# A four-layer graph network on one core: the gather lists are copied inside SBUF, and ScalarE takes over issues of SyncE

## What is computed

```
def _mp_layer(x, src_f, dst_f, ea_f, W, b):
    m = jnp.concatenate([x[dst_f], x[src_f], ea_f], axis=1) @ W.T + b
    agg = jax.ops.segment_sum(m, dst_f, num_segments=n)
    return jax.nn.relu(agg)
```

## Time and profile before

| | |
|---|---|
| runs shown | 19621.43, 19653.47, 19695.85 us; median 19653.47 |
| the profiled execution's own time | 19688.76 us |
| its span | 19687.0 us |
| TensorE clock granted, mean | 0.608 of full speed |
| busy | POOL 59%, PE 43%, DVE 24%, ACT 6% |
| first and last gather start | 723.4 us, 19640.2 us |

### The profile page before, as it was taken

One profiled execution on the slowest core, in us unless ns is written; L12 is line 12 of the kernel. 1 busy time (PEld: TensorE's weight loads), 2 busy tenths in 40 slices (PEclk: granted clock), 3 DMA queues, 4 the chain that ended last, 5 costly groups with the idle time before them and its releaser, 6 DMA issues.

```text
span 19687.0 us, 144709 instructions
## 1 busy us (share of the span) xinstructions
PE 8408.0 (43%) x34014; PEld 7081.4 (36%) x34014; DVE 4696.8 (24%) x7726; ACT 1131.3 (6%) x2610; POOL 11661.9 (59%) x11663
## 2 busy tenths in 40 slices
PE   7655555444443333334444443333323333333333
PEld 4334433333333333334444433333323333233333
DVE  4333333333342111112333321111111111211111
ACT  2101111000000000001111100000000000000000
POOL 0366665567776666655555556566556655466665
PEclk9877777677776555556766765555555555555555
DMA  4444444333332111113333321111111111111111
GB/s 195 153 127 151 151 143 139 110 99 99 100 100 59 27 30 30 29 37 90 91 91 92 92 57 24 23 24 24 22 27 24 24 23 23 26 24 26 26 26 25
DMA packets 1013134, 1320.33 MB, mean 67 GB/s; under 512 B 546589, under 2 KB 704574, under 8 KB 987470
## 3 DMA queue, kind: packets, MB, share of 16 engines
q0 software_dynamic: 426240, 764.57, 16.1%
q1 hardware_dynamic: 586830, 555.05, 8.8%
HBM read 970.98 MB, written 347.67 MB: 67 GB/s over the span
## 4 chain that ended last, share of the span: by engine, by line
another core or an unknown queue 55%; PE 16%; issue 15%; DVE 6%; POOL 3%; DMA 1%; SPq 1%; ACT 1%; DVEq 1%; ACTq 0%; POOLq 0%
PE PS L768 9%; PE PS L688 4%; POOL BIG L609 3%; DVE BIG L1366 1%; DVE OH L1353 1%; PE PS L801 1%; DMA AG<-acc 1%; PE PS L697 1%; PE PS L762 1%; DVE BIG L1373 1%; PE PS L675 0%; DVE BIG L1381 0%; ACT STG L969 0%; DVE XC L1221 0%
## 5 line engine op out<-in xcount | busy, mean ns | idle before, releaser
L768 PE MATMUL PS<-BIG,OH 128*128 128x64 f32 (+3 forms) x23310 | 5750.7, 427 | 3954.7 <-issue 1337.2
L609 POOL DMA_INDIRECT BIG<-t_mp,IDX x4995 | 4842.8, 970 | 3238.9 <-issue 1819.5
L768 PEld LDWEIGHTS PS<-BIG,OH 128*128 128x128 f32 x23310 | 5062.8, 295 | 4510.7 <-issue 2778.6
L609 POOL DMA_INDIRECT BIG<-t_cell,IDX x3330 | 3578.2, 1075 | 2546.6 <-issue 1799.1
L1353 DVE TENSOR_TENSOR OH<-REL,IOTA 128x640 f32<-128x640 f32 x2331 | 1902.3, 823 | 3537.9 <-remote 2841.7
L762 PE MATMUL PS<-STG,CARRY 128*128 128x64 f32 (+3 forms) x1554 | 554.2, 454 | 5100.0 <-ACT STG L969 3497.7
L609 POOL DMA_INDIRECT BIG<-t_p,IDX x1665 | 1618.0, 972 | 1192.9 <-issue 470.3
L762 PEld LDWEIGHTS PS<-STG,CARRY 128*128 128x128 f32 x1554 | 345.7, 277 | 5286.6 <-ACT STG L969 3460.7
L609 POOL DMA_INDIRECT BIG<-t_gcn,IDX x1665 | 1621.7, 974 | 1000.0 <-DMA IDX<-in_src 507.7
L1366 DVE TENSOR_TENSOR BIG<-BIG,COEF 128x1280 f32<-128x1280 f32 x666 | 990.7, 1488 | 511.9 <-DMA BIG<-t_cell,IDX 491.8
L801 PE MATMUL PS<-BIG 128*128 128x128 f32 x3330 | 585.0, 338 | 949.0 <-DVE BIG L1373 736.8
(11 more groups left out here) (148 smaller groups left out, 3345.1 us busy)
## 6 DMA issues: line engine op xcount, KB each, us to landing
t_cell<-BIG SPq DMA_DIRECT2D x198, 1280.0 KB, 4.5
BIG<-in_dst_row SPq DMA_DIRECT2D x333, 240.0 KB
BIG<-t_mp,IDX POOLq DMA_INDIRECT x4995
BIG<-t_cell,IDX POOLq DMA_INDIRECT x3330
BIG<-t_gcn,IDX POOLq DMA_INDIRECT x1665
BIG<-t_p,IDX POOLq DMA_INDIRECT x1665
BIG<-in_ef SPq DMA_DIRECT2D x333, 80.0 KB
BIG<-t_q SPq DMA_DIRECT2D x333, 48.0 KB
```

The source lines that it names most:

```text
L609: nc.gpsimd.indirect_dma_start(to[:, j, :], None, table, bass.IndirectOffsetOnAxis(ap=IDX[:, s // CHUNKS, at:at + 1], axis=0)).then_inc(ga ...
L768: last = nc.tensor.matmul(WIN[:, 0:out_w], OH[:, s % CHUNKS, j * P:(j + 1) * P], src[:, j, :], start=False, stop=(s % CHUNKS == CHUNKS - 1 ...
```

## The change

- `CELLS` and `SRCS`, two new SBUF tensors of 128 x 1665 int32, hold all lists: `CELLS` is written by DVE where the cell indices were written in place before, `SRCS` by one more load of the prologue.
- ACT copies 15 columns of them to `IDX` (`copy_list`), three groups ahead, behind the staging of the window whose group had the slot. POOL waits for one semaphore, `list_ready`. SP's list loads are gone from the fast passes, with their waits for the gathers.
- `store_window` moves from SP to ACT, directly behind `copy_list`.
- `load_mlp` moves from SP to ACT, behind the relu of the chunk before.
- SP keeps coefficients, edge attributes, and the node work.
- ACT runs the first and the last unit of each pass written out (`edged_units`), as it did in the first and the mlp pass.
- DVE's one-hots and products are as before; their second operands stay in SBUF.

```
-                        load_list(g + AHEAD, (gi + AHEAD) % UNIT)
-                    if kind == "mlp" and not (last and s + AHEAD >= SLOTS):
...
-                        load_mlp(at + AHEAD, (c + AHEAD) % CHUNKS)
-                    if kind == "mlp" and c == 1 and not (first and gi == 0):
-                        store_window(g - 1)
-                    if kind != "mlp" and c == 2:
-                        store_window(g)
+                        load_coefficients(g + AHEAD, (gi + AHEAD) % UNIT)
...
-                            pool.wait_ge(idx_in[s // CHUNKS], 16 * (ub + u + 1))
+                            pool.wait_ge(list_ready, gb + u * UNIT + s // CHUNKS + 1)
...
+                def store_window(g):
+
+                    act.wait_ge(win_staged, gb + g + 2)
+                    hold(act)
+                    at = act.value_load(WBASE[0:1, bass.ds(g * CHUNKS, 1)], min_val=0, max_val=z.nodes)
+                    act.dma_start(acc[bass.ds(at, P), :], STG[:, 0:acc.shape[1]]).then_inc(sums_landed, 16)
+
+                def copy_list(g, to):
+
+                    nc.scalar.activation(IDX[:, to, :], lists[:, bass.ds(g * TILES, TILES)], copy
+                                         ).then_inc(list_ready, 1)
+
+                def load_mlp(c, to):
+                    act.dma_start(RR[to][0:QW, :], t["dst_row"][0:1, bass.ds(c * CT * P, CT * P)]
+                                 .to_broadcast([QW, CT * P])).then_inc(rr_in[to], 16)
+                    act.dma_start(SZ[to][QW:P, :], t["ef"][:, bass.ds(c * CT * P, CT * P)]).then_inc(ef_in[to], 16)
+                    at = act.value_load(WBASE[0:1, bass.ds(c, 1)], min_val=0, max_val=z.nodes)
+                    act.dma_start(QM[to][0:QW, :], t_q[bass.ds(at, QW), :]).then_inc(q_in[to], 16)
...
                     if c == CHUNKS - 1:
                         stage_window(g)
+                        if not last:
+                            copy_list(g + UNIT, s // CHUNKS)
+                        store_window(g)
...
                 def mlp_body(u, s, first, last):
...
+                    if not (last and s + AHEAD >= SLOTS):
+                        at = u * SLOTS + s
+                        if not (first and s == 0):
+                            act.wait_ge(oht_ready, at)
+                            act.wait_ge(hid_done, at)
+                            hold(act)
+                        load_mlp(at + AHEAD, (s + AHEAD) % CHUNKS)
                     if s % CHUNKS == 0 and not (first and s == 0):
-                        stage_window(u * UNIT + s // CHUNKS - 1)
+                        g = u * UNIT + s // CHUNKS - 1
+                        stage_window(g)
+                        if not (last and s > 0):
+                            copy_list(g + UNIT, (s // CHUNKS - 1) % UNIT)
+                        store_window(g)
```

More of the change, by code:

```diff
@@ L230, in gnn_program @@
         gathered = [sem(f"gathered{s}") for s in range(SLOTS)]
-        idx_in = [sem(f"idx_in{s}") for s in range(UNIT)]
+        list_ready, idx_in = sem("list_ready"), sem("idx_in")
         coef_in = [sem(f"coef_in{s}") for s in range(UNIT)]
@@ L459, in fast_pass, with load_coefficients @@
                 kind, table, width, acc = passes[n]
[L460 to L467, removed]
+                gb = z.groups * n
+                def load_coefficients(g, to):
+                    sp.dma_start(COEF[:, to, :], coef_d[:, bass.ds(g * TILES * 4, TILES * 4)]
+                                 ).then_inc(coef_in[to], 16)
                     if n == 0:
@@ L470, in load_list @@
                                      [:, bass.ds(g * TILES * CAT_E, TILES * CAT_E)]).then_inc(ea_in[to], 16)
[L472 to L484, removed]
                 def body(u, s, first, last):
[L487 to L490, removed]
+                    c, gi = s % CHUNKS, s // CHUNKS
+                    g = u * UNIT + gi
+                    if kind == "spline" and c == 0 and not (last and gi + AHEAD >= UNIT):
                         if not (first and gi == 0):
[L492 to L498, removed]
+                            sp.wait_ge(prod_ready, CHUNKS * (gb + g))
+                            hold(sp)
                             if n == 0:
@@ L501, in body @@
                                 hold(sp)
[L502 to L514 removed]
+                        load_coefficients(g + AHEAD, (gi + AHEAD) % UNIT)
                 def node(s, k):
                     node_slot(n, s, k, CREDIT_STORE + 16 * (gb + (k + z.lag) * UNIT - 1))
[L519 to L520 removed]
+                if kind == "spline":
+                    for g in range(AHEAD):
+                        load_coefficients(g, g)
                 end_phase(n)
@@ L524, in fast_pass @@
                         sp.dma_start(QM[c][QW:P, :], t["mw1"][2 * F:2 * F + FEAT_E, :]).then_inc(sem("mwe_in"), 16)
[L525 to L529, removed]
+                if kind == "spline":
+                    edged_units(sp, body, node)
+                else:
+                    with sp.Fori(0, z.steps - TAIL) as k:
+                        for s in range(SLOTS):
+                            node(s, k)
                 tail_steps(lambda s, k: node_slot(n, s, k, CREDIT_STORE + 16 * (gb + z.groups)))
@@ L547, in body @@
                         hold(sp)
[L548 removed]
+                    sp.dma_start(IDX[:, 0, 0:1], lists[:, bass.ds(i, 1)]).then_inc(idx_in, 16)
                     if not first:
@@ L597, in fast_pass @@
                 kind, table, width, acc = passes[n]
-                cb, ub = z.chunks * n, z.units * n
+                cb, gb = z.chunks * n, z.groups * n
                 with pool.Fori(0, z.units) as u:
@@ L955, in fast_pass @@
                 cb, gb, ub = z.chunks * n, z.groups * n, z.units * n
+                lists = CELLS if kind == "spline" else SRCS
                 def copy_attributes(g, gi, u):
```

24 lines of the change are left out of this document (16 added, 8 removed).

## The result

The changed kernel takes **18965.75 us** (median of 3 runs, 18942.91 to 18981.92) against 19653.47: a ratio of 0.9647, 95% interval 0.9614 to 0.9681, so 688 us less. The prediction was 19400, 253 less. The direction was right and the time lies in the range, but the gain is 2.7 times the forecast.

What follows compares the result with a forecast made beforehand. POOL's gathers and its stops for index lists were taken as the bound. 19689 - 490 + 160 + 80 + 5 = 19444, less 35 for the median of runs: 19400 us; range 18600 to 20050, the forecast's own 18950 to 19550.

Steps and rivals of the forecast that it cites:

- What bounds the kernel: POOL's gathers, standing still for index lists: 2802 us in 280 stops, one being 6.8 us until the count, then 4.65.
- Lists by ACT's copy: Lists copied on ACT instead of loaded by SP: -490 us outside the mlp pass, +160 us in it.
- The 60% kept: Share of the 810 us from 222 shorter stops expected to remain, the rest lost to new stops; also applied to mlp.
- Store by ACT: 777 window stores, 1.26 us each, moved from SP to ACT behind the list copy, unseen by POOL: 0 us.
- Loads of the mlp pass by ACT: Three loads per chunk moved to ACT, 1.95 us, on the path at PE's 40 relu waits: +80 us.
- ACT's sequencer is slowed as SP's is: Rival: ACT issuing DMAs while POOL gathers becomes slow, mainly in mlp: 20340 us, or 20050 for mlp alone; chance 0.23 (with high mlp terms).
- Nothing is kept: Rival: PE's late counts set POOL's standing time, so shorter stops bring more stops: 19740 us, no change; chance 0.22.
- SP's slowness was the deadline: Rival: slow SP list loads cause the stops, and half of the 2802 us go: 18500 us; chance 0.13.
- The Trainium skill's rule: Issuing DMAs on several engines saves only sequencer time; only the list transfer counts, making the first term -215 us.
- More in number: Sign of being right: POOL's stops for lists become shorter but more numerous.
- shorter by 60 to 100 us each: Sign of being right: the time each sum pass loses.
- ACT's register instructions over 100 ns: Sign of being wrong, pointing to the rival of a slowed ACT sequencer.

Runs made afterwards that it cites:

- e1: Kernel before with only the list copies moved to ACT; window stores and mlp loads stay on SP: 19124.1 us, 0.9839 of the kernel before.
- e4b: Changed kernel plus two unread 1150-column copies on ACT between staging and list copy, on a chip with late counts: 19361.3 us, 0.9942 of the kernel before.
- e2: Changed kernel with only the window's store put back on SP: 19137.2 us, 0.9843 of the kernel before.
- e3: Changed kernel with only the mlp pass's loads put back on SP: 18840.3 us, 0.9697 of the kernel before.
- e10b: Changed kernel with the store on SP, in spline and sum passes issued behind the node step's load of the sums: 18869.3 us, 0.9696 of the kernel before.
- e0: The changed kernel run again, unaltered, as yardstick on another chip: 18848.2 us, 0.9688 of the kernel before.
- e6: Kernel before, with SP loading the list ahead of the previous group's store in spline and sum passes: 19031.0 us, 0.9665 of the kernel before.
- e7: Changed kernel plus two semaphore increments nobody waits for in each SP node slot: 19047.4 us, 0.9670 of the kernel before.
- e11b: Changed kernel with lists copied ahead of the staging except in the mlp pass, on a chip with late counts: 18523.4 us, 0.9516 of the kernel before.
- e11: Changed kernel with lists copied ahead of the staging except in the mlp pass, on the chip without stops: 16384.0 us, 0.9983 of the kernel before.

## Why the prediction was right or wrong

**What bounds the kernel: right.** POOL stands still for a list, and the two parts of a stop were 6.8 and 4.65 us; they became 6.7 and 1.00. What was not seen is that the first part comes in two lengths: 4.2 us are added where VectorE waits for a node product first.

**Lists by ACT's copy (-490 and, in the mlp pass, +160: together -330): right in sum, by luck.** e1 measured -317, and two errors cancel in it. The 60% kept was a guess from two windows; e4b gives 61% as a total, of passes that keep anything from less than nothing to twice the dose. What fell is the form of the give-back: it was to be "new stops", and there were fewer, not more (379 to 357). The mlp pass did not get longer (2754.8 to 2750.5), so its +160 was too high; then the -490 took too much as well, since e1's -317 is 39% of 810 and not 60. e4b's dose was laid over a kernel with the early load of the sums, e1 has the late one; whether that makes the difference wasn't tried, and on e1's chip there is no trace of the kernel before.

**Store by ACT (0): this is the step that failed.** "It stands behind the list's copy, so POOL doesn't see it" looked at ACT, where the store went, and costed its own 1.26 us. It did not look at SP's queue, which it left. There the load of the sums stood behind it, and behind that load VectorE, PE and the stop (followed in the last pass; in the others other transfers of SP stood behind it as well). e2 measured 289 us, e1 against e3 284, e10b got it back by order alone. With this term the sum would have been 19689 - 490 - 289 + 160 + 80 + 5 - 35 = 19120, and with the loads at 0, 19040.

**Loads of the mlp pass by ACT (+80): not there.** With the loads on ACT the time is 8 us more (e0 against e3) or 13 more (e2 against e1), which is no difference. In a gathering stretch of the changed kernel that began at 9235.89:

```profile
9241.16 0.32 ACTq L954 DMA_DIRECT2D BIG<-in_dst_row  x1
...
9241.58 0.39 ACTq L956 DMA_DIRECT2D BIG<-in_ef  x1
...
9242.74 0.33 ACTq L958 DMA_DIRECT2D BIG<-t_q  x1
```

1.91 us for the three, as estimated (1.95), where SP took 8.4. Over all 333 chunks the three take 1.97 us on average and 4.3 at most on ACT, and took 2.93 and 9.95 on SP in the kernel before. And PE's wait for ACT's relu fell, from 264.0 us in 40 waits, with 36.9 us in 8 more at the carry, to 181.6 us in 94:

```profile
PE PS L737 <- ACT BIG L963: 120.6, 53, 8.9
PE PS L731 <- ACT BIG L963: 61.0, 41, 2.8
```

So the rival "ACT's sequencer is slowed as SP's is" is refuted by its price: it needed about 6 us a chunk. Its premise is not quite wrong. The store's register row is as quick as before, but at the wait for the staging, where the kernel before had no instruction over 60 ns, the changed kernel has some of up to 708:

```profile
L946 ACTq FUSED_REGOPS  x777: 37/43/48, 754.5 to 18917.2; - x195
```
```profile
L967 ACTq FUSED_REGOPS  x537: 46/46/60, 3609.4 to 19655.0; - x179
```
```profile
L937 ACTq FUSED_REGOPS  x515: 3/43/708, 3610.6 to 18866.0; - x172
```

In all, 83 of ACT's 6167 such instructions took over 500 ns, against 278 of SP's 1611 in the same trace. Instructions of over 500 ns stand on ACT only in passes in which it issues DMAs: e2 and e10b, where it issues them in the mlp pass alone, have 55 and 47 sequencer instructions of ACT over 500 ns there and none in the other six passes, and the kernel before, e1 and e6, where ACT issues none, have none at all. So the earlier trace rows compared an ACT that issued nothing, as the prediction itself had warned.

**"Nothing is kept"** is refuted by e1 and e4b. **"SP's slowness was the deadline"** (18500) had a grain of truth: SP mattered, but by its order; e3 leaves it 999 slow loads, and e7 gives it more to do, without a price.

**The Trainium skill's rule** (DMA: Bandwidth & Descriptors, "Issuing engines are not separate DMA queues"), by which issuing on another engine saves only the sequencer's time, would have made the first term -215. The trace doesn't bear it out as a bound here: e2 shows 289 us for a move whose issue takes 0.34 us. It saves a place in an in-order queue. e10b agrees with the rule in one respect, that the engine itself is indifferent.

**The signs.** `IDX<-in_src` gone and ACT the releaser, 1.0 us after the staging: as said. Stops "7 to 8 us": 7.9 in the one shown, 6.8 on average (2417 / 357). "More in number": wrong. Mlp pass "no shorter than 2754 us": 2750.5. Sum passes "shorter by 60 to 100 us each": 141 to 178. Of the last pass's 141, 98 are the store's by e2 against e0. "ACT's register instructions over 100 ns", named as a sign of being wrong, did come (708), without the cost that was to go with them.

Open: what makes counts late on some chips; where the store's gain lies by pass (e2 is longer than e0 in spline 1, `t_gcn` and `t_mp` 3 by 167, 65 and 98 us, but shorter in `t_mp` 1 and 2, whose stops in e0 are often of the long kind, over 10 us, with the product mostly 25 us or more into the stretch). There the load of the sums comes 2 us after the restart as well, in 25 and 28 of 31 node steps of e0, so an early load alone doesn't make the product early. Only the last pass was followed by timeline. And which of SP's transfers behind the store costs the 167 us of spline 1: a run that moves the load of the sums alone would tell.

## What to carry to other kernels

When an instruction leaves an in-order queue, list what stood behind it there and who waits for that, before costing the instruction itself: here a 0.34 us store was worth 289 us by what stood behind it, in the last pass the next step's load, and putting the store behind that work on SP gave the same with the store still on SP. A wait row for that load (902 us on VectorE) was in the profile of before: read the waits of every engine on the chain, not only of the bound one. It points at the place, and gives no price. And where the chip makes handshakes late, take the shortest chain of them: POOL waiting for PE's count itself, and not for a copy behind a staging behind it, was worth another 346 us.

## What the hardware showed

- PE's counts are seen late while POOL issues gathers without a pause, on most of the chips used (7 to 41 us for the node products of the last pass; what isn't seen there when POOL stops is mostly seen 6 to 7 us after), and never on one of them. There the same kernel is 16% faster (16410 against 19441 to 19695 us). A tuning gain of 3.5% on the former is 0.2% on the latter.
- SP's register instructions at the store rise to 1396 ns on the former and stay at 37 to 48 ns on the latter. ACT's are slowed too, more rarely: at the wait for the staging up to 708 ns in the changed kernel and 1397 in e11b, and at most 60 in the kernel before and in e11 on the chip without stops. It comes only in passes in which ACT issues DMAs itself (e2: 55 sequencer instructions over 500 ns in the mlp pass, with 988 DMAs of ACT, and none elsewhere; before, e1 and e6: none). POOL's own register instructions stay under 200 ns in all traces looked at.
- In the last pass, products 21 us into a gathering stretch were seen before its end, 7 to 25 us later (e0, e10b); those at 23 to 27 us mostly in the stop, 37 us later and more (e2). In the first `t_mp` pass a product 5 us into a stretch was seen within 0.2 us (e0, e2, changed kernel). The time into the stretch isn't the whole of it: in the first `t_mp` pass of the changed kernel, 14 of 15 products 13.4 us into a stretch were seen 24 to 28 us later, when POOL had stopped.
